# Hop 1 and hop 0 of 25 pairs of graphs as one 512-column product, with hop 0's part summed in SBUF by VectorE

## What the kernel must compute

```
e          = leaky_relu(sj[:, None, :] + si[:, :, None] + ab, 0.2)      # scores from (X @ Wv + bv) @ aw
alpha      = A * exp(e)
transition = alpha / (sum(alpha, -1) + 1e-12)
H = 0; Xk = X
for k in 0, 1, 2:
    H  = H + Xk @ Wk[k] + bk[k]
    Xk = transition @ Xk
x   = layernorm(X + relu(H))
out = layernorm(x + (A @ x) @ w)
```

## Time and profile before

| | |
|---|---|
| median of 3 runs | 277.48 us (277.46 to 281.25) |
| the profiled execution | 277.04 us, of which the span in the profile is 275.2 us |
| busy share of the span | PE 98%, weight loads 96%, VectorE 77%, GpSimd 72%, ScalarE 69% |
| DMA | 34.92 MB, 58.1% of 16 engines' span |

### The profile page before, as it was taken

The page is one execution under the profiler, slowest core; times in us unless marked ns, Lnnn a source line. Parts: engine busy times, 40 slices in busy tenths (PEclk is TensorE's granted clock), DMA queues, the critical chain, the costliest instruction groups (busy, mean ns, idle before and its releaser), DMA issues.

```text
span 275.2 us, 6489 instructions
## 1 busy us (share of the span) xinstructions
PE 268.7 (98%) x2199; PEld 263.0 (96%) x2199; DVE 210.8 (77%) x562; ACT 188.8 (69%) x428; POOL 196.8 (72%) x420
## 2 busy tenths in 40 slices
PE   8999999999999999999999999999999999999992
PEld 4899999999999999999999999999999999999991
DVE  0787887877778787777878777787877777788874
ACT  2788866677766677776667777666777765666643
POOL 3565577778877777887777788777777777557574
PEclk9999999999999999999999999999999999999998
DMA  7955367957845585348585278556773394912304
GB/s 228 301 138 79 117 101 172 116 132 111 148 128 157 154 144 70 126 138 153 141 154 151 81 110 137 147 148 155 133 97 51 108 124 105 126 50 80 114 0 152
DMA packets 28614, 34.92 MB, mean 127 GB/s; under 512 B 7075, under 2 KB 16422, under 8 KB 28582
## 3 DMA queue, kind: packets, MB, share of 16 engines
q1 hardware_dynamic: 27872, 33.99, 58.1%
q10 hardware_dynamic: 710, 0.53, 0.6%
HBM read 26.09 MB, written 8.42 MB: 125 GB/s over the span
## 4 chain that ended last, share of the span: by engine, by line
PE 91%; DVE 3%; POOL 2%; DMA 1%; issue 1%; ACT 0%; DVEq 0%; POOLq 0%
PE ps_h L1004 24%; PE ps_v L1004 17%; PE ps_y L1004 15%; PE ps_out L1004 14%; PE ps_agg L1160 10%; PE ps_v L1100 3%; PE ps_v L1104 3%; PE ps_v L1102 3%; DMA WY_sb<-Wk_dram 1%; PE ps_agg L1004 1%; PE ps_y L1030 1%; PE ps_v L1030 1%; POOL rstd L877 1%; POOL res L888 0%; DVE WX_lo L817 0%
## 5 line engine op out<-in xcount | busy, mean ns | idle before, releaser
L642 DVE SCALAR_TENSOR_TENSOR ps_h<-ps_h,inv_rowsum,bias 128x256 f32<-128x256 f32 x60 | 26.5, 488 | 22.7 <-PE ps_h L1004 22.7
L901 POOL TENSOR_TENSOR XT_lo<-xt,XT_hi 128x512 fp32r<-128x512 f32 x32 | 41.5, 1300 | 3.0 <-ACT XT_hi L385 1.4
L913 POOL TENSOR_TENSOR alpha<-exps,adjs 128x256 f32<-128x256 f32 x31 | 22.9, 738 | 23.3 <-ACT exps L428 23.3
L1004 PE MATMUL ps_v<-WX_hi,XT_hi 128*128 128x256 f32 x128 | 36.7, 287 | 0.3 <-DVE ps_v L648 0.2
L1004 PE MATMUL ps_v<-WX_lo,XT_hi 128*128 128x256 f32 x128 | 36.0, 282 | 0.0
L1004 PE MATMUL ps_v<-WX_hi,XT_lo 128*128 128x256 f32 x128 | 36.0, 281 | 0.0
L1004 PE MATMUL ps_h<-WX_hi,XT_hi 128*128 128x256 f32 x124 | 35.0, 282 | 0.0
L1004 PE MATMUL ps_h<-WX_lo,XT_hi 128*128 128x256 f32 x124 | 35.0, 282 | 0.0
L1004 PE MATMUL ps_h<-WX_hi,XT_lo 128*128 128x256 f32 x124 | 34.9, 282 | 0.0
L459 ACT ACTIVATE y<-res,offset,rstd 128x256 f32<-128x256 f32 x62 | 33.6, 591 | 1.6 <-POOL offset L868 1.5
L917 POOL TENSOR_TENSOR alpha_lo<-alpha,alpha_hi 128x256 fp32r<-128x256 f32 x31 | 22.7, 733 | 15.9 <-ACT alpha_hi L437 15.9
(11 more groups left out here) (165 smaller groups left out, 915.5 us busy)
## 6 DMA issues: line engine op xcount, KB each, us to landing
xt<-xt_dram SPq DMA_DIRECT2D x32, 256.0 KB, 5.2
nodes<-nodes_dram SPq DMA_DIRECT2D x32, 256.0 KB, 5.7
out_dram<-out_sb SPq DMA_DIRECT2D x30, 256.0 KB, 5.0
adjs<-adjs_dram SPq DMA_DIRECT2D x32, 128.0 KB, 5.5
spread<-si_rows_dram SPq DMA_DIRECT2D x29, 128.0 KB, 4.7
W_sb<-Wk_dram SPq DMA_DIRECT2D x2, 256.0 KB, 3.8
si_rows_dram<-scores SPq DMA_DIRECT2D x29, 1.0 KB, 4.0
WY_sb<-Wk_dram ACTq DMA_DIRECT2D x1, 256.0 KB, 3.8
```

The costliest lines, as they stand in the source:

```text
L642: last = dve.scalar_tensor_tensor(ps_h[:, b], ps_h[:, b], inv_rowsum[k % 2][:, b:b + 1], bias[:], ALU.mult, ALU.add)
L901: pool.tensor_tensor(XT_lo[k % 7][:].rearrange("p c b i -> p (c b i)"), xt_sb[k % 4][:], XT_hi[k % 7][:].rearrange("p c b i -> p (c b i)") ...
L913: pool.tensor_tensor(alpha[:], exps[:], adjs_sb[k % 5][:], ALU.mult).then_inc(alpha_ready, 1)
L1004: last = pe.matmul(to, a, b, start=start and n == 0, stop=stop and n == 2, skip_group_check=True)
```

## The change

For pairs 2 to 26 (25 pairs) X W1 and X W0 are one product of 512 columns: `hops(k)` multiplies the same stationary tile with [W1, W0] laid side by side (the two halves of `WX_hi` and `WX_lo` change places) and writes the whole 512-float row of `ps_v`: V1 in columns 0 to 255, X W0 in 256 to 511. `hop0(k)` falls away for these pairs. The matmuls add into `ps_v`, in whose columns 256 and 257 the row sums stand, so VectorE clears these two columns once it has read them (`sums_cleared`). VectorE then takes X W0 plus the bias to SBUF (`x0`, into the new `hops_sum`), and adds alpha V1 times the inverse row sum there (`h_of`, in the place of `scale_h`). `residual1` reads `hops_sum` in the place of `ps_h` for these pairs. `propagate_v2` of the next pair also waits for `x0`, `propagate_v1` of the next pair for `h_of`. VectorE's order changes: `inverse` stands first, `residual1` with its statistics stands ahead of `residual2`, and `v1_lo` and `x0` follow `moments2_of`. For all pairs, `scale_v` signals each graph by itself, and `hop1` and `hops` wait for it graph by graph.

```diff
+        hops_sum = sb("hops_sum", [P, PER, D])
...
+        FIRST_BOTH = 2
+        def both_hops(k):
+            return FIRST_BOTH <= k < PAIRS - 5
+        def boths(k):
+            return k - FIRST_BOTH + 1
+        def hop0s(k):
+            return len([j for j in range(k + 1) if not both_hops(j)])
...
             def wx_hi(n):
                 act.wait_ge(Wk_loaded[n], DMA)
-                act.activation(WX_hi[:, :, n], (W0_sb, W1_sb)[n][:, :, 0:D], ACT.Copy).then_inc(WX_hi_ready[n], 1)
+                act.activation(WX_hi[:, :, 1 - n], (W0_sb, W1_sb)[n][:, :, 0:D], ACT.Copy).then_inc(WX_hi_ready[n], 1)
...
                 act.wait_ge(inv_ready, k + 1)
-                for b in range(PER):
-                    last = act.activation(ps_v[:, b, 0:D], ps_v[:, b, 0:D], ACT.Copy,
-                                          scale=inv_rowsum[k % 2][:, b:b + 1])
-                last.then_inc(v_scaled, 1)
+                if both_hops(k):
+                    act.wait_ge(sums_cleared, boths(k))
+                for b in range(PER):
+                    act.activation(ps_v[:, b, 0:D], ps_v[:, b, 0:D], ACT.Copy,
+                                   scale=inv_rowsum[k % 2][:, b:b + 1]).then_inc(v_scaled, 1)
...
                 dve.wait_ge(rowsum_ready, k + 1)
+                if both_hops(k):
+                    dve.memset(ps_v[:, :, D:D + 2], 0.0).then_inc(sums_cleared, 1)
                 dve.reciprocal(inv_rowsum[k % 2][:], rowsum[:]).then_inc(inv_ready, 1)
+            def x0(k):
+                dve.wait_ge(v1_done, k + 1)
+                dve.wait_ge(res1_ready, k)
+                dve.tensor_tensor(hops_sum[:], ps_v[:, :, D:2 * D], bias[:].unsqueeze(1).broadcast_to([P, PER, D]),
+                                  ALU.add).then_inc(x0_ready, 1)
+            def h_of(k):
+                dve.wait_ge(av1_done, k + 1)
+                dve.wait_ge(x0_ready, boths(k))
+                for b in range(PER):
+                    last = dve.scalar_tensor_tensor(hops_sum[:, b], ps_h[:, b], inv_rowsum[k % 2][:, b:b + 1],
+                                                    hops_sum[:, b], ALU.mult, ALU.add)
+                last.then_inc(h_ready, 1)
...
+                elif both_hops(k):
+                    dve.wait_ge(h_ready, boths(k))
                 else:
-                    dve.wait_ge(h_done, k + 1)
+                    dve.wait_ge(h_done, hop0s(k))
...
-                dve.scalar_tensor_tensor(res1[:], ps_h[:], 0.0, nodes_sb[k % 2][:],
+                dve.scalar_tensor_tensor(res1[:], hops_sum[:] if both_hops(k) else ps_h[:], 0.0, nodes_sb[k % 2][:],
                                          ALU.max, ALU.add).then_inc(res1_ready, 1)
...
-                else:
+                elif not both_hops(k):
                     scale_h(k)
                 inverse(k + 1)
+                if both_hops(k):
+                    h_of(k)
...
-                if there(k - 2):
-                    residual2(k - 2)
-                    statistics2(k - 2)
-                    moments2_of(k - 2)
                 residual1(k)
                 statistics1(k)
                 moments1_of(k)
                 if k == 0:
                     v2_lo(4)
-                v1_lo(k + 1)
+                if there(k - 2):
+                    residual2(k - 2)
+                if not both_hops(k + 1):
+                    v1_lo(k + 1)
+                if there(k - 2):
+                    statistics2(k - 2)
+                    moments2_of(k - 2)
+                if both_hops(k + 1):
+                    v1_lo(k + 1)
+                    x0(k + 1)
                 if there(k - 1) and there(k + 6):
                     aggregate_lo(k - 1)
...
+            def hops(k):
+                for b in range(PER):
+                    pe.wait_ge(v_scaled, PER * (k - 1) + b + 1)
+                    for c in range(C):
+                        last = product(ps_v[:, b], (XT_hi[k % 7][:, c, b], XT_lo[k % 7][:, c, b]),
+                                       [W[:, c].rearrange("p n d -> p (n d)") for W in (WX_hi, WX_lo)], False,
+                                       c == C - 1)
+                last.then_inc(v1_done, 1)
...
+                if both_hops(k - 1):
+                    pe.wait_ge(x0_ready, boths(k - 1))
...
+                elif both_hops(k - 1):
+                    pe.wait_ge(h_ready, boths(k - 1))
                 elif k < LAST:
                     pe.wait_ge(res1_ready, k)
...
-                if k > 0:
+                if k > 0 and not both_hops(k):
                     hop0(k)
-                hop1(k + 1)
+                if both_hops(k + 1):
+                    hops(k + 1)
+                else:
+                    hop1(k + 1)
```

More of the change, by code:

```diff
@@ L190, in resnorm_graph_kernel @@
         h_scaled = sem("h_scaled")
+        sums_cleared = sem("sums_cleared")
+        x0_ready = sem("x0_ready")
+        h_ready = sem("h_ready")
         res1_ready = sem("res1_ready")
@@ L582, in _ @@
             dve.wait_ge(WX_hi_ready[0], 1)
-            dve.tensor_tensor(WX_lo[:, :, 0], W0_sb[:], WX_hi[:, :, 0].bitcast(F32), ALU.subtract).then_inc(WX_ready[0], 1)
+            dve.tensor_tensor(WX_lo[:, :, 1], W0_sb[:], WX_hi[:, :, 1].bitcast(F32), ALU.subtract).then_inc(WX_ready[0], 1)
             def shift_of_scores():
@@ L816, in _ @@
             dve.wait_ge(WX_hi_ready[1], 1)
-            dve.tensor_tensor(WX_lo[:, :, 1], W1_sb[:, :, 0:D], WX_hi[:, :, 1].bitcast(F32),
+            dve.tensor_tensor(WX_lo[:, :, 0], W1_sb[:, :, 0:D], WX_hi[:, :, 0].bitcast(F32),
                               ALU.subtract).then_inc(WX_ready[1], 1)
@@ L1051, in hop1 @@
                     pe.wait_ge(WX_ready[1], 1)
-                pe.wait_ge(v_scaled, k)
                 for b in range(PER):
+                    pe.wait_ge(v_scaled, PER * (k - 1) + b + 1)
                     for c in range(C):
                         last = product(ps_v[:, b, 0:D], (XT_hi[k % 7][:, c, b], XT_lo[k % 7][:, c, b]),
-                                       (WX_hi[:, c, 1], WX_lo[:, c, 1]), False, c == C - 1)
+                                       (WX_hi[:, c, 0], WX_lo[:, c, 0]), False, c == C - 1)
+                last.then_inc(v1_done, 1)
+            def hops(k):
+                for b in range(PER):
+                    pe.wait_ge(v_scaled, PER * (k - 1) + b + 1)
+                    for c in range(C):
+                        last = product(ps_v[:, b], (XT_hi[k % 7][:, c, b], XT_lo[k % 7][:, c, b]),
+                                       [W[:, c].rearrange("p n d -> p (n d)") for W in (WX_hi, WX_lo)], False,
+                                       c == C - 1)
                 last.then_inc(v1_done, 1)
@@ L1063, in hop0 @@
                 elif k < LAST:
-                    pe.wait_ge(h_scaled, k)
+                    pe.wait_ge(h_scaled, hop0s(k) - 1)
                 for b in graphs:
@@ L1069, in hop0 @@
                         last = product(ps_h[:, b] if k < LAST else last_h[:, b], (XT_hi[k % 7][:, c, b], XT_lo[k % 7][:, c, b]),
-                                       (WX_hi[:, c, 0], WX_lo[:, c, 0]), k == 0 and b == 0 and c == 0, c == C - 1)
+                                       (WX_hi[:, c, 1], WX_lo[:, c, 1]), k == 0 and b == 0 and c == 0, c == C - 1)
                     if k == LAST:
```

## The result

The changed kernel takes 275.19 us (274.89 to 275.33, 6 runs) where the kernel before takes 277.56 in the same series: ratio 0.9914, 95% interval 0.9899 to 0.9929. That is 2.4 us, and the forecast was 6.5. The sign and the absence of a new wait in the steady state were right; the size of the one term that carries the sum was not.

What follows compares the result with a forecast made beforehand. TensorE, never waiting in the steady state, was taken as the bound. Joining saves 0.26 us a pair, 6.5 us over 25 pairs: 277.04 less 6.5 is 270.5, plus 0.44 to the median gives 271.0; range 269.8 to 276.5.

Steps and rivals of the forecast that it cites:

- What bounds the kernel: Steady state: TensorE never waits, busy 40.00 of 40 us, so only shortening its instruction list can shorten the kernel.
- the term of 0.26 us a pair: TensorE: 12 matmuls of 512 columns at 0.217 take 2.60 us instead of 2.86; 6.5 us over 25 pairs.
- the floor of the weight load: TensorE: weight load of 128 x 128 sets about 0.11 to 0.12 us a matmul, with 256 columns just below it.
- the upper one: Upper bound for a 512-column matmul: excess comes from reading fp32r columns and doubles, 0.238 us, gaining nothing.
- The argument from the 2-column instructions: Eight fp32 instructions of 2 columns take 0.108 us each with almost nothing to stream, read as the weight load's floor.
- VectorE's chain: VectorE from inverse to v1_lo: 5.09 to 5.14 us, v1_lo ending at 7.51, 0.28 ahead of TensorE's need at 7.79.
- GpSimd and SBUF: residual1, now reading two SBUF tensors, falls mostly in GpSimd's gap; overlap with alphas 0.1 to 0.2 us, counted as nothing.
- A hold of VectorE by `XT_lo`: Slower rival: GpSimd's XT_lo holds residual1 for 1.30 us in every pair, costing 20 us, 297 in all; chance 0.09.
- Edits at nothing: Edits priced at zero: scale_h off hop0's path, swapped WX halves, more scale_v signals, residual1 earlier and residual2 later.
- rival 1: TensorE: a float32r column costs more than its cycle, 0.225 to 0.238 us a matmul; 273.5 to 277.5 us; chance 0.22.
- 25 x 12 x 0.002: Gain by the Trainium skill's gap rule, two 256-column matmuls becoming one of 512; given as 0.7 us.

Runs made afterwards that it cites:

- e1: Changed kernel with each 512-column product issued as two of 256, VectorE's part kept: 277.9 us, ratio 0.9999 to the kernel before.
- e3: Kernel before plus 8 groups of 24 extra matmuls behind its last, other engines idle: float32r 234 ns at 512 columns, 120 at 256; bf16 219 and 112.
- e5: Kernel before plus extra matmul groups at its end, varying format and data: bf16 real data 216 ns at 512 columns, float32r on ones 228.
- e4: Changed kernel with residual2 and its statistics ahead of residual1 again: 275.7 us, ratio 0.9915 to the kernel before.
- e2: Kernel before with only scale_v signalling each graph and hop1 waiting graph by graph: 276.98 us, ratio 0.9969.
- e6: The changed kernel run again, nothing altered: 275.15 us, ratio 0.9902 to the kernel before.
- e7: Changed kernel with the joined product only from pair 12 on (FIRST_BOTH = 12): 276.64 us, ratio 0.9954 to the kernel before.
- e9: Changed kernel with small terms of products with X in bf16 from pair 9 on and no joined product: 273.29 us, ratio 0.9845 to the kernel before.

## Why the prediction was wrong

- **What bounds the kernel** was right: the chain is TensorE before and after, and e1 shows that nothing else moved the steady state.
- **The price of a 512-column matmul is the step that failed, the term of 0.26 us a pair.** The prediction read the excess of a 256-column matmul over streaming as the floor of the weight load, so that it would vanish behind 512 columns, and took 0.217 from the row of plain fp32 "with the same array time and a weight load". It measures 0.234, in the pipeline and alone (e3). The floor exists (112 in e3 for 128 columns), but a float32r column costs 0.445 ns, so 256 of them already take longer than the floor (120), and the excess doubles almost wholly with the columns. The row that I called nearest was of another format: plain fp32 does take 216 (e5), and float32r doesn't. The bound that came out nearly right is the upper one, "a matter of reading fp32r columns, not of the weight load", 0.238. The term is 0.06 to 0.08 a pair in the place of 0.26, and 25 pairs make 1.5 to 2.0 us. Why a float32r column costs more than a bf16 one stays open.
- **The argument from the 2-column instructions** (0.108 each) was sound as to the floor and wrong as a reason: a floor of 0.108 to 0.112 doesn't explain 0.119, and I let 8 ns pass as nothing. 12 times 0.017 over 25 pairs is 5.1 us, a little more than the whole miss.
- **VectorE's chain** was right in order and a little pessimistic: `v1_lo` had 0.69 of cover where 0.28 was forecast, 0.18 of which is the longer period. The rest is that the memset costs next to nothing (0.06, and within the reciprocal) and that `inverse` starts 0.07 earlier. `scale_v` had 0.36 in the place of 0.17.
- **GpSimd and SBUF**: `residual1` fell in the gap as forecast. e4 shows that the exclusion is real, and that its direction was harmless there. The row that the prediction set against it (`residual1` at 132.34 "in spite of" an `alphas` up to 132.35) shows nothing, since the two overlap by 0.01. In the changed kernel it starts 0.25 behind the end of GpSimd's normalisation, where an overlap of 0.1 to 0.2 was forecast. A hold of VectorE by `XT_lo` wasn't tried.
- **Edits at nothing**: the signal for each graph was not nothing. In four late steps TensorE waited about 0.11 for `scale_v` (e2), which the prediction, looking at one pair in the middle, didn't see; without these waits the late part is 0.40 shorter. The rest of the change gives that back. In the trace e1 is 0.48 behind e2 at the last group: 0.10 ahead of the first `propagate_v1`, 0.10 up to pair 3, nothing from there to the first late step, and 0.29 in the late part. This last is there wherever `hop0` of pair 26 is done a step earlier: the late part takes 34.8 in e1, e6, e7 and the changed kernel, and 34.5 in e2 (e4 has 34.5 too, but its gap stands just ahead). TensorE then comes to the late steps sooner, and ahead of one `propagate_v2` the 6 matmuls of `project` and a gap take 1.07 where the kernel before has 0.79: in the changed kernel that `propagate_v2` starts at 250.74, and GpSimd's `alpha_lo` (249.86, 0.73) ends at 250.59. That TensorE waits for it is read from these times and from the kernel, not tried. So the gain of 1.89 us at the last group in the traces is 2.04 of joining and 0.33 of signals, less 0.48.
- **The rivals**: rival 1 is what happened, and its 273.5 to 277.5 holds the result; it had 0.22. The range of 269.8 to 276.5 held the time only because it took in most of rival 1; the forecast's own 270.0 to 272.3 didn't.
- **A slip in a sum**: 25 x 12 x 0.002 is 0.6 and not 0.7. The forecast didn't use it.

## What to carry to other kernels

Joining two products with the same stationary operand saves only what a matmul costs beside its columns, and that must be measured in the very format: take the distance at two widths above the floor and draw the line, before pricing a third. Here it was 5 to 7 ns of 239 for two float32r matmuls, which pays only if the new operation on another engine falls where that engine has room, as VectorE had. Where a product is split in terms, the terms that need few bits can go in the format with the cheapest column: that gave more here (e9) than the joining. As a change of format cost some 15 ns in e5, equal formats were kept together; another order wasn't tried in the kernel.

## What the runs showed of the hardware

- Distances between the starts of matmuls with a weight load of 128 x 128 each, at the 2.4 GHz level: float32r 112, 120, 177, 234 ns for 128, 256, 384, 512 columns; bf16 109 and 216 for 256 and 512 with real data, 112 and 219 with ones from a constant; plain fp32 of 256 columns 216 for each of its two instructions. The Trainium skill, in "TensorE: Matmul & The Clock Gate", section Back-to-back issue gap, gives 262 and 518 cycles for 256 and 512 columns, as the gap of a matmul by itself (109 and 216 ns at 2.4 GHz): bf16 with real data follows it to the nanosecond here, with a weight load for each matmul, and float32r doesn't.
- A change between float32r and bf16 and back costs some 15 ns (0.680 against 0.666 us at 512 columns, 0.353 against 0.338 at 256, e5).
- Float32r of 512 columns with ones on both sides takes 228 ns in the place of 234 (e5).
- A memset of 2 x 2 columns in PSUM takes 0.06 us, the shortest VectorE operation in these traces.
- Of two instructions with SBUF operands on VectorE and GpSimd that overlap, the later one is longer, by 0.22 of 0.35 (GpSimd, e4) and 0.36 of 0.50 (VectorE). In the setup of the kernel before, an `XT_lo` that starts at 8.79, while VectorE splits weights until 9.15, takes 1.49 in the place of 1.29: GpSimd loses 0.20 of 0.36.
